# Part of layer 1's adjacency product made in layer 0: three matmuls more per strip there, 36 turns fewer in layer 1

## The reference, cut to what matters

```python
# layer 0
XW = mobius_matvec(W, X)
gamma = 2.0 / maximum(1.0 - sum(XW * XW), EPS)
nominator, denominator = A_hat @ (gamma * XW), clamp_abs(A_hat @ (gamma - 1.0))
... row-wise mobius scaling, relu, expmap0; it needs A_hat.sum(-1) too
x = layernorm(x + that)
# layer 1
a_hat = adj + eye; d = sum(a_hat, 1) ** -0.5
x = layernorm(x + ((a_hat * d[:, None] * d[None, :]) @ x) @ W.T + b)
# layer 2: degree-normalised diffusion plus softmax(beta * cosine similarity * adj) @ x
# layer 3: (adj @ x) into a GRU cell
```

## Time and profile before

| | us |
|---|---|
| median of three runs (lowest, highest) | 1423.76 (1414.07, 1426.44) |
| the profiled execution: its time, its span | 1423.67, 1421.9 |
| mean granted clock, as a share of 2.4 GHz | 0.974 |
| TensorE busy in matmuls, in weight loads | 1312.5, 1018.2 |
| VectorE, ScalarE, GpSimd busy | 1084.8, 1059.4, 577.8 |

### The profile page before, as it was taken

One profiled execution on the slowest core, in us unless ns is written; L12 is line 12 of the kernel. 1 busy time (PEld: TensorE's weight loads), 2 busy tenths in 40 slices (PEclk: granted clock), 3 DMA queues, 4 the chain that ended last, 5 costly groups with the idle time before them and its releaser, 6 DMA issues.

```text
span 1421.9 us, 21055 instructions
## 1 busy us (share of the span) xinstructions
PE 1312.5 (92%) x7640; PEld 1018.2 (72%) x7640; DVE 1084.8 (76%) x1943; ACT 1059.4 (75%) x1369; POOL 577.8 (41%) x441
## 2 busy tenths in 40 slices
PE   5999999999988989998899999999999879999995
PEld 5999999999976767773466666666665658666663
DVE  6855556555668989998888887988888878777874
ACT  6887887788777667775688878788797557667663
POOL 4312222222454533343377767777776640000010
PEclk9899999999999999999899999999999999999998
DMA  9999999999957868894688778787786849877850
GB/s 306 377 387 331 357 359 353 339 357 360 339 222 256 321 242 323 328 373 160 238 274 308 267 269 314 271 297 290 245 320 204 281 172 422 325 267 264 297 183 22
DMA packets 114808, 413.08 MB, mean 291 GB/s; under 512 B 10000, under 2 KB 23568, under 8 KB 90128
## 3 DMA queue, kind: packets, MB, share of 16 engines
q1 hardware_dynamic: 106256, 407.54, 79.0%
q10 hardware_dynamic: 8448, 4.20, 1.0%
HBM read 340.40 MB, written 71.30 MB: 290 GB/s over the span
## 4 chain that ended last, share of the span: by engine, by line
PE 52%; DVE 19%; ACT 16%; issue 7%; POOL 5%; DMA 1%; POOLq 0%; ACTq 0%; DVEq 0%; SPq 0%
DVE part_l L1346 6%; PE strip_b L596 5%; PE acc L541 5%; PE acc L532 4%; PE acc L533 4%; PE acc L513 3%; PE mid L513 3%; ACT arena L755 3%; DVE part_l L1225 3%; PE acc L613 3%; PE acc L610 2%; PE acc L611 2%; PE strip_b L493 2%; ACT part_h L810 2%; ACT part_h L762 2%
## 5 line engine op out<-in xcount | busy, mean ns | idle before, releaser
L1346 DVE TENSOR_TENSOR part_l<-arena,part_h 128x1024 fp32r<-128x1024 f32 x256 | 327.0, 1313 | 60.6 <-ACT part_h L810 59.4
L1059 POOL TENSOR_TENSOR part_l<-arena,part_h 128x512 fp32r<-128x512 f32 x237 | 304.4, 1298 | 152.2 <-ACT part_h L848 152.2
L810 ACT ACTIVATE part_h<-arena 128x1024 fp32r<-128x1024 f32 x256 | 265.4, 1055 | 125.9 <-PE acc L541 113.0
L1225 DVE TENSOR_TENSOR part_l<-arena,part_h 128x1024 fp32r<-128x1024 f32 x128 | 161.0, 1266 | 124.2 <-ACT part_h L762 123.6
L848 ACT ACTIVATE part_h<-arena 128x512 fp32r<-128x512 f32 x256 | 157.7, 623 | 95.3 <-DVE arena L1428 94.7
L532 PE MATMUL acc<-part_h,Y 128*128 128x512 f32 x512 | 220.5, 431 | 5.5 <-ACT part_h L810 3.0
L533 PE MATMUL acc<-part_h,Y 128*128 128x512 f32 x512 | 203.8, 398 | 0.0
L1027 POOL TENSOR_TENSOR sc<-sc,power 128x4 f32<-128x4 f32 x32 | 49.4, 1543 | 330.0 <-DVE sc L1251 330.0
L596 PEld LDWEIGHTS strip_b<-ident,arena 128*128 128x128 f32 x1024 | 126.8, 142 | 69.2 <-DVE arena L1428 19.6
L541 PE MATMUL acc<-part_l,Y 128*128 128x512 f32 x512 | 164.5, 403 | 10.1 <-DVE part_l L1346 9.7
L596 PE MATMUL strip_b<-ident,arena 128*128 128x128 f32 x1024 | 156.6, 276 | 15.7 <-DVE arena L1428 11.2
(11 more groups left out here) (258 smaller groups left out, 2786.8 us busy)
## 6 DMA issues: line engine op xcount, KB each, us to landing
arena<-adj_t SPq DMA_DIRECT2D x128, 1024.0 KB, 4.9
arena<-in_adj SPq DMA_DIRECT2D x64, 1024.0 KB, 8.2
adj_t<-arena SPq DMA_DIRECT2D x64, 1024.0 KB, 7.6
arena<-in_adj SPq DMA_DIRECT2D x128, 512.0 KB, 5.9
part_h<-adj_t SPq DMA_DIRECT2D x64, 512.0 KB, 5.1
part_l<-adj_t SPq DMA_DIRECT2D x64, 512.0 KB, 5.2
scratch<-v ACTq DMA_DIRECT2D x8, 256.0 KB, 10.2
arena<-scratch SPq DMA_DIRECT2D x8, 256.0 KB, 5.2
```

What stands on the lines that cost most here:

```text
L810: act.activation(flat(part_h[:, slot:slot + 2, :]), turned_pair(n), ACT.Copy).then_inc(high_done, 1)
L1059: pool.tensor_tensor(part_l[:, b % 4, :], mixed[b % G_SLOTS], part_h[:, b % 4, :].bitcast(F32), ALU.subtract).then_inc(low_done, 1)
L1225: dve.tensor_tensor(flat(part_l[:, slot:slot + 2, :]), full_pair(n), flat(part_h[:, slot:slot + 2, :]).bitcast(F32), ALU.subtract).then_in ...
L1346: dve.tensor_tensor(flat(part_l[:, slot:slot + 2, :]), turned_pair(n), flat(part_h[:, slot:slot + 2, :]).bitcast(F32), ALU.subtract).then_ ...
```

## The change

Slab s of layer 0 (s = 2 to 7) also multiplies its first `fused(s)` = 1, 2, 3, 4, 4, 4 groups by layer 1's input, whose groups 0 to 3 are made while slabs 1 to 4 run. That is 18 groups, 72 strips. These strips are left out of layer 1, which has 92 turns instead of 128 (slabs of 16, 16, 14, 12, 10, 8, 8 and 8 turns). Layer 0 takes the groups of slabs 2 to 7 in the order 0, 4, 1, 5, 2, 6, 3, 7. The partial sums are read out beside layer 0's, written to DRAM, loaded in layer 1 and added to the `eye` buffer. The two halves of layer 0's sums are now added by VectorE as it reads PSUM, and no longer by POOL. The bias is added to `x_nat` itself, right after `eye_share`. To make room, `mx` lies where `x_nat` does (so `x` is loaded a second time in slab 1), and the unit rows are written to two small buffers and moved to their place by a DMA on ScalarE's queue, which `score` waits for.

```diff
+FUSED = 4
+def fused(s):
+    return min(FUSED, max(s - 1, 0))
+GROUPS0 = [list(range(GROUPS)) if s < 2 else [0, 4, 1, 5, 2, 6, 3, 7] for s in range(SLABS)]
+INPUTS1 = [0, 4, 1, 5, 2, 3] + [SLABS - 2, SLABS - 1]
+TURNS1 = [(s, 2 * g + h) for s in range(2) for g in INPUTS1[:-1] for h in range(2)] \
+    + [(s, 2 * INPUTS1[-1] + h) for s in range(2) for h in range(2)] \
+    + [(s, m) for s in range(2, SLABS) for m in range(2 * fused(s), PAIRS)]
+ROWS_FROM = {1: [TURNS1.index((s, PAIRS - 1)) + (9 if s == 1 else 1) for s in range(SLABS)],
+INPUTS_LATER = {1: 3, 4: 6, 26: 7}
-HOOKS = {1: 15, 3: 26}
+HOOKS = {1: 16, 3: 26}
@@ multiply0 (TensorE) @@
+                if g == s - 2 and g < FUSED and m % 2 == 0:
+                    pe.wait_ge(y1_low_done, g + 1)
+                        if both:
+                            if start:
+                                pe.matmul(sums, h, planes[:, :, j, :], start=True, stop=False)
+                            pe.matmul(sums[:, 0:3:2, :], low, planes[:, 0:3:2, j, :], start=False, stop=False)
+                            if not start:
+                                pe.matmul(sums, h, planes[:, :, j, :], start=False, stop=False)
+                            last = pe.matmul(sums[:, 2, 0:D], h, y1_low[:, j, :], start=False, stop=False)
@@ score (TensorE) @@
-                    if e < 3:
-                        pe.wait_ge(row[1], row_done(1, 2 * e + 1, "unit_low"))
-                        pe.wait_ge(row[0], row_done(1, 2 * e, "unit_low"))
+                    if e < 3 or e == 7:
+                        pe.wait_ge(units_in[1], 16 * (e % 4 + 1))
+                        pe.wait_ge(units_in[0], 16 * (e % 4 + 1))
@@ layer 2's loop (TensorE at step 10; VectorE has k = 14 at step 8) @@
+                if n == 10:
+                    rows1(12, SLABS - 2)
@@ read_acc0 (VectorE) @@
-                dve.tensor_copy(nat[:, 2, :], acc0[2][:, 0:YW])
-                dve.tensor_copy(nat[:, 3, :], acc0[3][:, 0:YW]).then_inc(acc_read, 1)
+                for n in range(2):
+                    parts = both0(n)[:, :, 0:2 * LO].rearrange("p q (h w) -> p q w h", w=LO)
+                    if n == 1 and s >= 2:
+                        dve.wait_ge(partial_half, s - 1)
+                    dve.tensor_reduce(sums_of[s % 2][:, 2 * n:2 * n + 2, :], parts, AX.X, ALU.add
+                                      ).then_inc([sums_half, acc_read][n], 1)
@@ ScalarE @@
+            def y1_parts(g):
+                act.wait_ge(y_scaled, g + 1)
+                act.activation(y1_high[:, Q * g:Q * (g + 1), :], by_block(turned[g % 2][:]), ACT.Copy).then_inc(y1_high_done, 1)
+            def read_partial(s):
+                act.wait_ge(product, slab_product(0, s))
+                if s >= 4:
+                    act.wait_ge(partial_out[s % 2], partials_at(s - 2))
+                act.activation(partial(s)[:, 2:4, :], both0(1)[:, :, 2 * LO:2 * LO + D], ACT.Copy).then_inc(partial_half, 1)
+                act.wait_ge(sums_half, s + 1)
+                act.activation(partial(s)[:, 0:2, :], both0(0)[:, :, 2 * LO:2 * LO + D], ACT.Copy).then_inc(partial_read, 1)
+                if k == 15:
+                    act.wait_ge(row[s % 2], row_done(1, s, "unit_low"))
+                    act.dma_start(halves_of[:, s, :, :].bitcast(F32), unit_new[s % 2]).then_inc(units_in[s % 2], 16)
+                if m == PAIRS - 1 and 1 <= s <= FUSED:
+                    y1_parts(s - 1)
@@ POOL, eye_share and layer 1's loop; in layer 0 it has y_scale(s - 1) at m = 14, y1_parts(s - 1) at m = 15 @@
+                pool.tensor_tensor(by_block(eye[s % 2]), x_nat[:, mine, :], wide(dcol[:, mine]), ALU.mult).then_inc(made, 1)
+                pool.wait_ge(made, count)
+                pool.tensor_tensor(x_nat[:, mine, :], x_nat[:, mine, :],
+                                   bias1[:].unsqueeze(1).to_broadcast([P, Q, D]), ALU.add).then_inc(biased, 1)
+            def add_partial(s):
+                pool.wait_ge(eye_scaled, s - 1)
+                pool.wait_ge(partial_in[s % 2], partials_at(s))
+                pool.tensor_tensor(eye[s % 2], eye[s % 2], turned[s % 2][:], ALU.add).then_inc(eye_in, 1)
-                if k == 0:
-                    before("x_bias")
-                    pool.tensor_tensor(v[:], x_nat[:, mine, :],
+                if n in INPUTS_LATER:
+                    y_low(1, INPUTS_LATER[n])
+                    if n == ROWS_FROM[1][s] - 3 and s >= 2:
+                        add_partial(s)
```

More of the change, by code:

```diff
@@ L315, in groups_loaded @@
         def groups_loaded(l, n):
-            before = sum(i % TURNED_SLOTS == n % TURNED_SLOTS for i in range(GROUPS * SLABS)) if l == 3 else 0
+            before = sum(i % TURNED_SLOTS == n % TURNED_SLOTS for i in range(STEPS1 // 2)) if l == 3 else 0
             return 16 * (before + n // TURNED_SLOTS + 1)
@@ L668, in _ @@
                 multiply0(n)
-            for n in range(TURNS_ALL):
+            for n in range(STEPS1):
                 for k, s in hooks(1, n):
@@ L690, in _ @@
                         rows2(m % NB, m // NB - 1)
-            for n in range(TURNS_ALL):
+            for n in range(STEPS3):
                 if n < PAIRS // 2:
@@ L697, in _ @@
                 multiply(3, n)
[L698 removed]
+            for n in range(STEPS3, STEPS3 + HOOKS[3]):
                 for k, s in hooks(3, n):
@@ L1120, in _ @@
                     y_low(3, (m - 6) % NB // 4)
-            for n in range(TURNS_ALL + HOOKS[3]):
+            for n in range(STEPS3 + HOOKS[3]):
                 if n < PAIRS // 2:
```

328 lines of the change are left out of this document (206 added, 122 removed).

## The result

The changed kernel takes 1423.15 us (median of 20 runs, 1417.45 to 1429.09), the kernel before beside it 1420.08 (20 runs, 1412.66 to 1426.6): ratio 1.0028, 95% interval 1.0015 to 1.0041. It is slower by some 4 us (2 to 6 by the interval), far less than 1%; the forecast was 8 us slower. The intervals of this study are 0.3 to 0.5% wide, so that differences of that size can be told here. The profiled execution has a span of 1425.2 us against 1421.9. Both profiled executions are some 4 us above their medians (1423.67 against 1420.08, 1427.01 against 1423.15). So single differences of a few us between two profiles are read only where the stretch repeats in others.

A forecast was written before the change was run, and what follows sets the result against it. The prediction took TensorE to bound layer 0, and TensorE and VectorE both layer 1. Its terms, 52 - 12 + 3.5 + 1.5 + 2 - 46 + 2 + 6 = +9 on 1423.67, gave 1432 us, range 1404 to 1453.

The forecast's parts named there:

- The triple: Layer 0: 288 couples of matmuls become three matmuls (260, 390, 128 columns), 0.41 us each, 0.18 more than now: +52 us.
- rival (1): Faster: in layer 0 columns alone count (+35 for +52), in layer 1 lost turns give -59 for -46; 1403 us, chance 0.22.
- The triple's stated upper bound: Layer 0: with 0.019 us of fixed cost for each matmul, a triple adds 0.193 us, +56 in all.
- Layer 1's short slabs: Layer 1: 17.0 us for 8 turns, 19.2 for 10, 21.5 for 12, 23.2 for 14, against 25.57: -38.5.
- The second load of x: Layer 0: 2 MB loaded again, 6 us of a nearly full DMA, behind four slots of lead: +1.5 us (0 to 5).
- the overlap with TensorE's waits: Layer 0, slabs 4 to 7: TensorE's present waits hide about 3 us a slab of added work: -12 (bounds -6 and -14).
- The change of slab: Layer 0: two VectorE reduces make each change 1.4 us and not 0.91; seven changes and the last read: +3.5 (0 to +8).
- `y1_parts`: Layer 0, end of slabs 1 to 4: ScalarE waits for POOL's `y_scale`, 0.5 us each: +2 (0 to 6).
- the bias, -7.5: Layer 1: bias in place removes the 5.11 us wait behind POOL's bias and the slow clock after it: -7.5 (-3 to -9).
- the seam, +6 and +2: POOL work ahead of `y_low(7)`, +2 (0 to 5); layer 1's end waiting for unit rows and ScalarE, +6 (0 to +10).
- (2): Slower: layer 1's short slabs wait for POOL's list, a slab costs 6 us more than 17: +18, 1450 us, chance 0.26.
- (3): Layer 0: the DMA sets the pace, matmuls hide 8 us more, reloading `x` costs 6: +6, 1429 us, chance 0.07.

The follow-up runs named there:

- c1_no_third: The changed kernel with the third matmul of each triple left out, so one cross product is missing from the moved strips: ratio 0.9858 to the kernel before.
- b1_bias: The kernel before with only the bias added to `x_nat` by POOL right behind `eye_share`, no groups moved: ratio 0.9964 to the kernel before.
- a4_y1_later: The changed kernel with the input parts of groups 1 to 3 made two pairs later, in the next slab of layer 0: ratio 0.9970 to the kernel before.
- n4_early: The changed kernel with groups in natural order, partial sum added six turns before a chain's start, slab 1's chain two turns earlier: ratio 1.0000 to the kernel before.
- a3_tail: The changed kernel with slab 6's unit rows transposed at step 6 of layer 2 and not at 10: ratio 1.0003 to the kernel before.
- a1_add_early: The changed kernel with the partial sum added six turns before a chain's start and not three: ratio 0.9992 to the kernel before.
- a2_rows_38: The changed kernel with slab 1's chain in layer 1 started two turns earlier: ratio 0.9978 to the kernel before.

## Why the prediction was right or wrong

**What held.** That it comes out a little slower, and within 1%. The triple: 0.41, so +52 stands against rival (1)'s 0.353, and c1_no_third shows the narrow matmul paid in full. The triple's stated upper bound doesn't come out of what it names (388 columns at 2.4 GHz and 0.019 for one more matmul are 0.181, not 0.193); nothing rests on it. Layer 1's short slabs: 18.9 for 10 turns (569.29 to 588.21) where I had 19.2, and 17.6, 17.2 and 16.7 for 8 turns where I had 17.0, with VectorE busy 17.06 of 17.57. The second load of x: 1.5 is not contradicted; the runs can't tell it from nothing.

**What failed: three terms of the sum had the wrong size.** Layer 0 came to +38.3 (+37 counted from the span's start), not +47. The first and largest miss is the overlap with TensorE's waits, put at -12, 3 for each of slabs 4 to 7, with -14 as its bound; some 20 was hidden. Slabs 4 to 6 got triples and a longer change worth 9.5, 12.0 and 12.0 us and grew by 5.5, 9.3 and 7.7, so they hid 4.0, 2.7 and 4.3: the rule "3 a slab" held for them. Slab 7 got 11.5 (its last read is no longer than before) and grew by 2.8: it hid 8.7. The rule was read off slab 3 and carried to slab 7, where ScalarE, VectorE and POOL also make layer 1's input, and where the waits of 6.5 us and the slow clock went, as shown above. How much is hidden depends on the execution as well: slabs 4 and 6 took 48.35 us in the profile of before, with the slow clock behind the wait of 1.64, and 46.72 to 46.75 in b1_bias, where the clock stayed up behind the same wait. The change of slab came to +5.2 and not +3.5. Slabs 1 to 3 grew by 12.8, of which their triples are 8.6 and their longer changes 2.7; the rest, 1.5, is what the second load and `y1_parts` came to beyond the waits of before, where I had +3.5. Yet `y1_parts` could be placed 4.5 us better (a4_y1_later): where it stood, it kept up a wait that the triples could have hidden.

The second is the bias, -7.5. I had its wait go with no other in its place. b1_bias measures 4.3 in that stretch: ScalarE's read of the sums, behind the writing of slab 1's rows, was already 2.2 us late under the bias's shadow. In the changed kernel, where slab 2 has 14 turns and the two chains are only six turns apart, this successor is 3.28, and slab 3 took 29.56 us where my terms give 33.5 - 7.5 - 4.1 = 21.9. Slab 2 came out 1.4 better than my terms. So layer 1 gave -40.6 and not -46.

The third is the seam, +6 and +2. `y_low(7)` cost about 0.5 (first eye matmul 52.8 us after the layer's start, 52.3 before), and the unit rows' DMA didn't hold TensorE in the changed kernel: it lands in 3.8 us, and slab 7's weight product starts 3.3 us after the eye matmul where it was 2.7. (In n4_early and c1_no_third the score matmuls ahead of that product wait 1.33 and 1.58 us for something the profile doesn't name, which may be this DMA.) The seam is 44.9 and not 41.5, +3.4. The ScalarE part that was foretold is 1.9 of it, by a3_tail; the rest isn't split. Not in the sum at all are another 3.4 us between layer 2's first transposition and the end. Of these 2.4 lie at the start of layer 3, from its first matmul to TensorE's wait of 2.7 us for VectorE: 15.5 us and not 13.1, with a granted clock of 0.80 and not 0.99. a1_add_early, a3_tail and a4_y1_later take 15.3 to 15.5 there at 0.81 or 0.82, a2_rows_38 takes 14.1 at 0.89; what decides the clock there was not settled.

Check: 38.3 - 1.1 (the earlier start) - 40.6 + 3.4 + 3.4 = +3.4 against the spans' +3.3. In the prediction 47 - 46 + 8 = +9. That the forecast is no further off is in part luck: I had layer 0 8.7 too high and the seams 4.6, but layer 1's gain 5.4 too large, and the 3.4 at the end not at all.

**The rivals.** (1), 1403, fell with the triple. (2), 1450, didn't happen as a time, but its mechanism is real: POOL's partial sum is late twice in the changed kernel (2.91 and 3.71 us), and with two groups it is late in four slabs in a row and costs 2.1 to 3.6 us in the three of them that can be compared (25.4, 25.2 and 23.9 against 21.8). The point from which it decides, as I put it (POOL's power ends after the last turn has begun), fits the 3.71: the power ends at 604.35, and TensorE had been ready for the eye matmul since 602.07. It misses the others. In slabs of 12 turns `add_partial` stands behind the unit rows too, and it is late for that. (3) is not supported: the DMA's share fell from 0.96 to 0.89 in slab 6 while the slab grew.

The Trainium skill, TensorE: Matmul & The Clock Gate, section "Back-to-back issue gap" (N / 2.4 GHz + 2.5 ns), gives 0.056 for the narrow matmul alone. The same section says that this is too low for few columns behind a weight load, and has about 0.081 for a stream of 128-column matmuls with their loads. Measured here with its load the narrow one costs 0.105, above both. The Trainium skill, SBUF — State Buffer, section "Who interferes with whom", has the loser blocked fully; the subtractions of VectorE are held half as long as that (17.06 us of VectorE in the 8-turn slab, where 5.8 in place of 2.8 in my sum of 16.2 would give 19.2), while its smallest steps do look blocked, below.

## What to carry to other kernels

Work moved into another stage costs what that stage's own waits don't cover: read those waits slab by slab, the last slab above all, since here it hid 8.7 of 11.5 us where its neighbours hid 3 to 4. When a stall is taken away, look at what was already late underneath it, for only the difference is gained, and when a loop body gets shorter, place again every step of another engine that was placed by turns: here the two placements in layer 1 took the kernel with two groups from 1.0115 to 1.0004, and with the one in layer 0 the changed kernel from 1.0028 to 0.9924, while the moving itself gained nothing.
